# The last batch's routing two to four places later in the tile loop, and the first expert tile turned before the last attention store

## The reference

```
x = x + attention(layernorm(x))            # causal, 16 heads, then W_proj and b_proj
n = layernorm(x)
logits = n @ Wg                            # 8 experts
two largest logits -> softmax over the two -> gate score, times alpha
out = sum over experts e of  comb[:, e] * (gelu(layernorm(n; ln_w[e], ln_b[e]) @ fc1_w[e] + fc1_b[e]) @ fc2_w[e] + fc2_b[e])
x = x + out                                # fc1 128 -> 512, fc2 512 -> 128
```

## Time and profile before

| What | us |
|---|---|
| Median of the timed runs | 540.84 |
| Span of the profiled execution, first to last instruction | 560.3 |
| PE busy in it | 473.9 (85%) |
| DVE busy | 373.1 (67%) |
| POOL busy | 366.1 (65%) |
| ACT busy | 322.9 (58%) |

### The profile page before, as it was taken

One profiled execution on the slowest core, in us unless ns is written; L12 is line 12 of the kernel. 1 busy time (PEld: TensorE's weight loads), 2 busy tenths in 40 slices (PEclk: granted clock), 3 DMA queues, 4 the chain that ended last, 5 costly groups with the idle time before them and its releaser, 6 DMA issues.

```text
span 560.3 us, 11807 instructions
## 1 busy us (share of the span) xinstructions
PE 473.9 (85%) x3296; PEld 277.1 (49%) x3296; DVE 373.1 (67%) x1316; ACT 322.9 (58%) x661; POOL 366.1 (65%) x712
## 2 busy tenths in 40 slices
PE   3379999999999998998898988786992999999930
PEld 1134443543443453443444443364981888888920
DVE  4588878889889889889889997741543521222226
ACT  2137786776676776676676666752550555565610
POOL 5956676586986986987887876955556444445520
PEclk9589999999999999999999999897996899999985
DMA  2323133134233234234224212276642685666439
GB/s 62 93 57 105 65 93 109 58 105 118 68 101 117 78 87 129 73 91 130 75 66 130 71 40 79 79 236 213 219 159 86 213 264 180 216 194 187 154 129 328
DMA packets 52726, 70.83 MB, mean 126 GB/s; under 512 B 11063, under 2 KB 38430, under 8 KB 52662
## 3 DMA queue, kind: packets, MB, share of 16 engines
q1 hardware_dynamic: 47478, 59.19, 34.7%
q0 software_dynamic: 4320, 8.53, 4.5%
q10 hardware_dynamic: 864, 2.36, 1.2%
HBM read 36.49 MB, written 20.94 MB: 102 GB/s over the span
## 4 chain that ended last, share of the span: by engine, by line
PE 51%; DVE 17%; issue 8%; POOL 6%; SPq 5%; DMA 4%; another core or an unknown queue 4%; ACT 3%; ACTq 0%; DVEq 0%; POOLq 0%
PE acc_bank L748 10%; PE slots L739 10%; PE slots L648 7%; PE acc_bank L680 7%; PE slots L665 5%; SPq L496 4%; DVE masked L940 3%; PE misc L616 3%; POOL z_dram L1235 2%; DVE z L893 2%; DVE row_max L934 2%; POOL probs L1252 2%; DMA y_in<-y_dram 2%; PE slots L644 2%
## 5 line engine op out<-in xcount | busy, mean ns | idle before, releaser
L811 ACT ACTIVATE probs<-slots 128x512 f32<-128x512 f32 (+1 forms) x352 | 185.6, 562 | 86.0 <-PE slots L665 79.2
L940 DVE CUSTOM_DVE_ANT_0 masked<-slots,causal_row 128x512 bf16<-128x512 f32 (+1 forms) x256 | 148.9, 614 | 20.8 <-PE slots L648 20.7
L648 PE MATMUL slots<-stack_k,stack_q 125*128 125x256 bf16 (+3 forms) x512 | 128.5, 307 | 19.4 <-DVE row_max L940 7.5
L1252 POOL TENSOR_SCALAR_AFFINE_SELECT probs<-probs 128x128 f32<-128x128 f32 (+2 forms) x352 | 116.1, 350 | 41.3 <-ACT probs L811 37.4
L665 PE MATMUL slots<-stack_q,stack_k 128*128 128x256 bf16 (+3 forms) x512 | 125.6, 301 | 2.9 <-DVE row_max L934 1.5
L1282 POOL DMA_INDIRECT y_dram<-y,z_in x71 | 69.7, 982 | 73.4 <-DVE y L1126 56.8
L841 ACT ACTIVATE hidden<-slots,w_in 128x256 f32<-128x256 f32 (+1 forms) x156 | 63.1, 455 | 82.6 <-PE acc_bank L748 29.2
L680 PE MATMUL acc_bank<-probs,v 128*32 128x512 f32 (+3 forms) x1024 | 95.6, 447 | 3.4 <-POOL probs L1252 2.7
L648 PEld LDWEIGHTS slots<-stack_k,stack_q 125*128 125x128 bf16 x512 | 48.3, 99 | 95.4 <-DVE row_max L940 49.7
L1235 POOL DMA_INDIRECT z_dram<-z,pos x64 | 63.6, 994 | 32.1 <-DVE pos L1034 17.7
L748 PE MATMUL acc_bank<-hidden,w_in 128*128 128x256 f32 (+1 forms) x312 | 73.0, 376 | 7.8 <-issue 4.0
(11 more groups left out here) (168 smaller groups left out, 523.1 us busy)
## 6 DMA issues: line engine op xcount, KB each, us to landing
w_in<-in_wpack SPq DMA_DIRECT2D x39, 516.0 KB
o_dram<-oT SPq DMA_DIRECT2D x32, 256.0 KB, 2.3
stack_k<-parts SPq DMA_DIRECT2D x95, 64.0 KB
stack_q<-parts SPq DMA_DIRECT2D x93, 64.0 KB
z_in<-z_dram SPq DMA_DIRECT2D x32, 132.0 KB
xt<-in_x SPq DMA_DIRECT2D x8, 256.0 KB, 3.7
onT<-o_dram SPq DMA_DIRECT2D x8, 256.0 KB
o_inv<-inv_dram SPq DMA_DIRECT2D x8, 256.0 KB
```

The source lines that it names most:

```text
L648: mm = pe.matmul(cols[:, i, :], q[0:K1, hh, blk * P:blk * P + P], k[0:K1, hh, 0:w], start=len(heads) == 1, stop=True, skip_group_check=True)
L811: act.activation(probs_of(n), columns(n, slot), ACT.Exp, scale=SCALE).then_inc(s_exp, 1)
L940: dve.tensor_tensor_reduce(out=masked[:, n % MASKED, 0:w], in0=slots[:, slot, 0:w], in1=causal_row[:, T - w:T], scale=1.0, scalar=NEG, op0 ...
L1252: pool.affine_select(out=diag, in_=diag, compare_op=ALU.is_ge, fill=0.0, base=0, pattern=[[0, len(heads)], [1, P]], channel_multiplier=-1) ...
```

## The change

The stages of the last batch (7) stand later in the tile loop, by two places (`o_scale`, `proj`, `r_stats`, `r_agg`, `r_root`), three (`o_spread` and all from `r_z` to `dispatch`) or four (`o_invert`). The parts of the table stand three to four places later, and part 2 stands ten places behind part 1 in place of five. `turn_z` of tile 0 moves from the end of the list in front of the loop into the attention part, at `n = 382`: behind the last `pv` and the PE part of batch 6's `rank`, and in front of `pv_out` 31. The list in front of the loop loses its leading `load 2`, so that `o_load` of batch 7 comes in front of the loads of tiles 2 and 3. No instruction is added or removed.

```
+TURN_FIRST = 382
...
+    at(TURN_FIRST, "turn_z", 0)
...
-            7: {"o_load": -1, "o_invert": 0, "o_spread": 2, "o_scale": 8, "proj": 10, "r_stats": 11, "r_agg": 11, "r_root": 11,
-                "r_z": 13, "zT": 15, "gate": 17, "r_top": 18, "r_exp": 19, "r_copy": 16, "r_comb": 21, "rank": 22,
-                "dispatch": 23}}
-    LATE_SMALL = 5
-    LATE_OTHER = {"t_count": 28, "t_span": 29, "t_owner": 30, "t_expert": 32, "t_row": 33, "pad_rows": 28}
+            7: {"o_load": -1, "o_invert": 4, "o_spread": 5, "o_scale": 10, "proj": 12, "r_stats": 13, "r_agg": 13, "r_root": 13,
+                "r_z": 16, "zT": 18, "gate": 20, "r_top": 21, "r_exp": 22, "r_copy": 19, "r_comb": 24, "rank": 25,
+                "dispatch": 26}}
+    LATE_SMALL = 10
+    LATE_OTHER = {"t_count": 31, "t_span": 32, "t_owner": 34, "t_expert": 35, "t_row": 37, "pad_rows": 31}
...
-    add(("load", EARLIEST), *placed.pop(-1, []), *(("load", i) for i in range(EARLIEST + 1, AHEAD)), ("turn_z", 0))
+    add(*placed.pop(-1, []), *(("load", i) for i in range(EARLIEST, AHEAD)))
```

## The result

The changed kernel takes 544.94 us (median of 4 runs, 543.3 to 546.37), against 540.92 us before (4 runs, 540.76 to 541.39). The ratio is 1.0067, 95% interval 1.0045 to 1.009: 4.0 us slower. The forecast was 544.0. The profiled execution after has a span of 541.2 us and a time of 543.3, so some 2.1 us lie around a span. It is the fastest of the four runs, 1.6 us under their median, so its rows show less than the whole loss. It has no hole, where that of before had two.

What follows compares the result with a forecast made beforehand. PE was taken to bound the tile loop at 3.89 us a tile. Seam 3.9 plus clock 1.3 minus norm 1.6 minus table 0.5 gave +3.1 on 540.84: 544.0 us, likeliest range 542.2 to 546.0, overall 540.2 to 546.6.

Steps and rivals of the forecast that it cites:

- hole: Profile of before, 376.4 to 387.0 and 420.4 to 433.8: PE largely idle; both cost some 20 us, hardly in timed runs.
- the likeliest case: Whole kernel: the four parts sum to +3.1 us, 544.0 us; own range 542.2 to 546.0, chance 0.57.
- Part 1: Seam, SP and ACT: late oT and store delay tile 2's tokens, PE waits 3.9 us, bounds 3.3 to 4.6.
- oT later by 2.8 us: Sign expected in the changed kernel's profile: ACT's copy oT runs behind hdnT and 2.8 us later.
- Part 2: Behind tile 2's wait: granted clock falls to half level, costing 1.3 us, bounds nothing to 3.4.
- Part 3: Batch 7's norm: later places remove PE's wait at zT 7, gain 1.6 us, bounds nothing to 3.3.
- At nothing: Moves of pad_rows' stores, o_invert and o_spread on SP, o_scale, and batch 7's dispatches: all costed at zero.
- o_scale stands two places later, which covers it: o_invert and o_spread behind loads 4 and 5 on SP: no cost; if uncovered, yT 3 and turn_y 3 held some tenths.
- Part 4: Table on DVE between yT 10 and yT 11: spreading it removes PE's turn_y wait, gain 0.5 us, bounds 0 to 1.2.
- the change does nothing, since the holes stand in the timed runs too and cover tile 2's wait: Rival for the tile loop: no change, 540.8 us; counted within the 0.13 chance of ending within 0.2%.

Runs made afterwards that it cites:

- seam alone: Kernel before with turn_z 0 in the attention part and o_load 7 in front of load 2, all places old: 545.88 us against 541.27, ratio 1.0089.
- o_load first alone: Kernel before with only load 2 moved behind o_load 7, turn_z 0 and oT as before: 543.53 us against 541.27, ratio 1.0050.
- places alone: Kernel before with only the later places of batch 7 and the table, list in front of the loop as before: 541.31 us against 541.27, ratio 1.0018.
- load 2 first: Full change, but load 2 stays in front of o_load 7: 543.32 us against 540.82 for the kernel before, ratio 1.0043.
- table alone: Kernel before with only the new places of the table and pad_rows: 540.54 us against 540.82, ratio 0.9996.
- the one look at before: Kernel before, unedited, run once more for a profile without holes: 541.27 us on one chip, 540.82 on the other.

## Why the prediction was right

**Time.** 544.94 against 544.0, +4.0 against +3.1, inside the likeliest case's own range.

**Part 1, the seam (3.9, bounds 3.3 to 4.6): right in mechanism; the time of turn_z 2 was right, the wait was not.** The links show. The axis is shifted by 368.56 - 367.77 = 0.79 us. Tile 2's tokens were forecast to be issued at 376.1, that is 375.3 on the new axis, and were at 374.61. Their landing took 4.1 us, not 3.0. turn_z 2 started at 378.77, against 378.3 forecast. The landing was thus over the upper bound of 3.7 from the rows, and the earlier issue made up for most of it. The estimate from the Trainium skill (DMA: Bandwidth & Descriptors, Anatomy of one DMA) was further off, at 2.3 us; the page gives it for DMAs that GpSimd issues, and these are SP's. The wait that PE shows is 2.51 us in the full change and 3.01 in seam alone, both under the lower bound of 3.3, because the step let PE come to tile 2 as in a profile whose tile 0 ran at full level (3.75 us); here tile 0 took 5.43, so PE came 1.7 us later. With these 1.7 the wait would be 4.2, inside the bounds. Seam alone measured 4.6 to 4.8, the clock behind its wait included. "oT later by 2.8 us" in the last paragraph mixed a start with an end: it started 368.69 + 0.79 - 367.33 = 2.15 us later.

**Part 2, the clock (1.3): a size that some runs have and the profiled one has not.** The fall behind the wait is seen in seam alone and in o_load first alone, where the stretch behind it was at 0.50, a loss of up to 1.7 us. In the full change's profile there was none: 0.89 of 3.40 us of work, then 1.00. A stretch at the lower level stood in tile 0 before the wait, and as PE would have waited for the tokens anyway, 1.7 us of that loss were hidden. The step priced the clock behind the wait and left out the clock in front of it, which takes away from what a wait costs. The sentence cited from the Trainium skill (TensorE: Matmul & The Clock Gate, What's actually happening) agrees with the windows of two kernels, 1.10 and 0.35 us of work in a stretch at 1.00, then 0.50; the full change's own profile does not show a fall. Of its four runs the two slower (545.37 and 546.37 us) had a mean granted clock of 0.958 and 0.957, the two faster 0.970 and 0.971; but in seam alone the slowest run had 0.973, so this does not decide what the slower runs lose.

**Part 3, zT 7 (-1.6): not delivered.** The step "the timed runs before should have a wait of 1.6 us that the hole hides" holds at most where tile 0 runs at full level. In the one clean profile of before it did not, and the margin was 0.26 us. The power and its place on POOL were sized well: z at 393.4 forecast, 393.55 measured on an axis 0.5 us later. What was wrong is PE's arrival at zT 7, put at 391.8 from a tile 0 at full level. And the places had a cost that was put at nothing.

**At nothing: wrong for o_invert and o_spread.** "o_scale stands two places later, which covers it" failed, and it was not yT 3 and turn_y 3 that paid: proj 7 waits 0.52 us in the full change, 0.90 with places alone and 1.05 with load 2 first. Putting o_invert to r_root back shortened the loop by 1.1 us. The change puts two SP stages behind two loads of over 2 us each, and the step counted only the two places given on DVE.

**Part 4, the table (-0.5): right in mechanism, a little large.** Two waits of 0.24 and 0.21 became one of 0.26. The loop of table alone is 0.3 us shorter; its median can't be told from before's.

**The sum.** That 3.9 + 1.3 - 1.6 - 0.5 came near is in part luck: two errors cancel in part. The places gave some 2 us less than forecast, and the seam, clock included, cost some 0.5 us less than 5.2. The two profiles without holes, the full change against the one look at before, split the 3.1 us by which its loop is longer: +2.7 in tile 1 (6.62 us from fc1 to fc1 in place of 3.89, the wait for tile 2's tokens), +0.7 at proj 7, -0.4 at the table, and nothing at zT 7. The remaining 0.9 us of the measured +4.0 stand in no profile. That the full change (+4.0) lies under seam alone (+4.6) does not show a gain of the places: the two intervals overlap, and the difference of the two loops (75.1 and 76.9) is about the 1.7 us that the lower clock behind seam alone's wait costs.

**The holes.** The prediction concluded that timed runs hardly have them. That is right for the chips on which the change was compared. On another chip every profile has them and every run is about as long (558.76 to 566.91 us over all kernels), and what the rival "the change does nothing, since the holes stand in the timed runs too and cover tile 2's wait" said is what was measured there: 0.9991. The holes are thus not a matter of the one profiled execution (560.48 us there, against a median of 562.2). Whether they belong to the chip or to its state at the time was not separated.

## What to carry to other kernels

When a stage moves in a list that several engines walk, follow each engine's copy of the queue: here the early transpose gained PE nothing, but put a copy behind a wait on ACT, a store behind the copy, and a load behind the store on SP. Here a queue reordered at a seam was paid at the first consumer without slack, and moving a store and a reload behind two loads was not covered by giving their consumer two places. Compare the length of the loop that the change touches as well as whole spans, and ask of every wait removed what else (another engine's time, a stretch at the lower clock) was hidden in it.

## What the runs showed of the hardware

- The same kernel takes 541 us on two chips and 562 us on a third. The difference lies in two stretches in which PE, ACT, DVE and SP lose time together while POOL's scatters keep their pace of 1.27 us: ACT is idle for up to 12.4 us, and the eight stores of `pad_rows` take SP 17.06 us in place of 8.21. Not every instruction is slow in them: DVE's chain for the table runs through the second at its usual 0.2 us a step. Before has them from 376.4 and 420.4, 4 us behind the first of eight scatters issued back to back (372.40 and 416.35) in both cases; the attention part, where the scatters stand 2 us or more apart, has none. The cause stays open.
- In that state a loss elsewhere may be free: the full change, 4.0 us slower on one chip, is within 0.2% of before on the other, with its wait for tile 2's tokens (1.97 us) still there.
- Eight of the nine profiles without holes have a stretch at half the clock in tile 0, whatever the kernel. It costs 1.7 us there (5.44 against 3.75 us from fc1 to fc1), and by the working in part 2 none of it where PE would have waited behind it.
- The landing of 132 KB of rows took 4.1 us, when 516 KB of weights had been issued 0.6 us before it on the same queue.
